# A macaron MoE–attention–MoE kernel: prefix sums in the other working bank, one more turn, and three operations moved between engines

## What is computed

```python
def ffn(x):                       # 8 experts of 384, 2 chosen per token, and one shared expert
    normed = layernorm(x) * ln_gamma + ln_beta
    logits = normed @ router_w.T
    top_v, top_i = top_k(softmax(logits), 2)
    gates = softmax(top_v)
    comb = sum(one_hot(top_i, 8) * gates[..., None], axis=1)
    out = sum(comb[:, e, None] * swiglu(normed, gate_up_w[e], down_w[e]) for e in range(8))
    return out + swiglu(normed, shared_gate_up_w, shared_down_w)

def attn(x):                      # windows of 128 tokens
    q, k, v = x @ Wq.T + bq, x @ Wk.T + bk, x @ Wv.T + bv
    scores = q @ k.T / sqrt(128)
    attn = softmax(where(in_top_32(scores), scores, -inf))
    r = leaky_relu(attn @ v) + x
    return layernorm(r) * gamma + beta

x = x + 0.5 * ffn(layernorm(x))
x = x + attn(layernorm(x))
x = x + 0.5 * ffn(layernorm(x))
```

## Time and profile before

| | us |
|---|---|
| median of three runs | 585.45 |
| span of the profiled execution, first to last instruction | 581.5 |
| median less span | 3.95 |
| PE busy | 500.6 (86%) |
| DVE busy | 388.7 (67%) |
| ACT busy | 330.0 (57%) |
| POOL busy | 332.0 (57%) |

### The profile page before, as it was taken

The page is one execution under the profiler, slowest core; times in us unless marked ns, Lnnn a source line. Parts: engine busy times, 40 slices in busy tenths (PEclk is TensorE's granted clock), DMA queues, the critical chain, the costliest instruction groups (busy, mean ns, idle before and its releaser), DMA issues.

```text
span 581.5 us, 14497 instructions
## 1 busy us (share of the span) xinstructions
PE 500.6 (86%) x3928; PEld 458.6 (79%) x3928; DVE 388.7 (67%) x1688; ACT 330.0 (57%) x792; POOL 332.0 (57%) x491
## 2 busy tenths in 40 slices
PE   2588999989999989999977499996899999799781
PEld 1466999979899989998974369794889989799780
DVE  5558864732558989879887958999785624222574
ACT  3367556565467777667753357673655546555430
POOL 2273766875565675356674405664566765565542
PEclk9989999999999999999977569997999999999996
DMA  6944858766886554766412254431668767676993
GB/s 184 316 112 167 261 188 237 243 233 239 284 260 218 190 187 173 258 226 205 155 47 59 69 195 176 160 112 54 209 224 257 248 221 246 228 262 237 322 320 124
DMA packets 88012, 117.82 MB, mean 203 GB/s; under 512 B 11848, under 2 KB 60880, under 8 KB 87936
## 3 DMA queue, kind: packets, MB, share of 16 engines
q1 hardware_dynamic: 76208, 96.75, 49.8%
q0 software_dynamic: 9312, 19.16, 9.5%
q10 hardware_dynamic: 2416, 0.99, 0.7%
HBM read 26.57 MB, written 26.19 MB: 91 GB/s over the span
## 4 chain that ended last, share of the span: by engine, by line
PE 52%; SPq 15%; ACT 9%; DMA 7%; issue 7%; DVE 5%; POOL 3%; ACTq 1%; POOLq 0%; DVEq 0%
PE ps_y L730 12%; PE ps_g L716 11%; PE ps_u L721 6%; SPq L441 6%; PE ps_h L721 5%; DMA xin<-rows 5%; SPq L484 4%; SPq L479 3%; PE ps_x L711 2%; PE w L630 2%; SPq L499 2%; POOL rows L1572 2%; ACT zz L849 2%; PE w L660 2%; PE w L616 2%
## 5 line engine op out<-in xcount | busy, mean ns | idle before, releaser
L1589 POOL DMA_INDIRECT results<-raw_gu,idx x163 | 164.6, 1010 | 144.8 <-ACT raw_gu L929 103.1
L1572 POOL DMA_INDIRECT rows<-zz,s_idx x128 | 126.0, 984 | 66.9 <-issue 28.3
L730 PE MATMUL ps_y<-dn_t,raw_gu 128*128 x978 | 139.2, 279 | 5.7 <-ACT raw_gu L929 5.0
L716 PE MATMUL ps_g<-x_t,raw_dn 128*128 128x128 f32 x978 | 137.5, 277 | 0.0
L730 PEld LDWEIGHTS ps_y<-dn_t,raw_gu 128*128 128x128 f32 x978 | 123.4, 193 | 9.3 <-issue 8.5
L716 PEld LDWEIGHTS ps_g<-x_t,raw_dn 128*128 128x128 f32 x978 | 122.8, 192 | 3.6 <-issue 3.5
L929 ACT COPY raw_gu<-ps_y 128x128 f32<-128x128 f32 x163 | 42.9, 263 | 103.5 <-PE ps_y L730 101.8
L923 ACT ACTIVATE sil<-ps_g 128x384 f32<-128x384 f32 x163 | 80.1, 491 | 22.0 <-PE ps_g L716 20.8
L920 ACT ACTIVATE x_t<-ps_x,bf_c,gf_c 128x128 f32<-128x128 f32 x163 | 75.3, 462 | 19.6 <-PE ps_x L711 19.4
L1397 DVE TENSOR_TENSOR raw_gu<-sil,ps_u 128x384 f32<-128x384 f32 x82 | 44.9, 548 | 54.2 <-PE ps_u L721 47.2
L1397 DVE TENSOR_TENSOR raw_gu<-sil,ps_h 128x384 f32<-128x384 f32 x81 | 44.5, 550 | 50.8 <-PE ps_h L721 35.9
(11 more groups left out here) (172 smaller groups left out, 729.0 us busy)
## 6 DMA issues: line engine op xcount, KB each, us to landing
raw_dn<-gu_t SPq DMA_DIRECT2D x163, 384.0 KB
xin<-rows SPq DMA_DIRECT2D x163, 64.5 KB
yg<-results SPq DMA_DIRECT2D x15, 512.0 KB, 5.1
results<-raw_gu,idx POOLq DMA_INDIRECT x163
rows<-pads SPq DMA_DIRECT2D x40, 64.5 KB
rows<-pads SPq DMA_DIRECT2D x5, 451.5 KB
rows<-zz,s_idx POOLq DMA_INDIRECT x128, 2.4
out<-xres SPq DMA_DIRECT2D x7, 256.0 KB, 3.3
```

Of the source, the lines that this page charges most:

```text
L716: t = pe.matmul(ps_g[k][:, c, :], ws[:, k4, c * P:(c + 1) * P], x_t[:, k, :], start=True, stop=True)
L730: t = pe.matmul(ps_y[:, 0, :], h_t[:, k4, c * P:(c + 1) * P], dn[:, bass.ds(off + c * D, D)], start=(c == 0), stop=(c == FC - 1))
L1572: pool.indirect_dma_start(xs, bass.IndirectOffsetOnAxis(s_idx[n][:, c, k:k + 1], 0), zz[n][:, k, c, :], None).then_inc(scat[n], 16)
L1589: pool.indirect_dma_start(yt, bass.IndirectOffsetOnAxis(idx[:, ky:ky + 1], 0), yb[:, ky, :], None).then_inc(yst[ky], 16)
```

## The change

- **Prefix sums.** Those of the first two steps go to bank `w0` (step 0 in its last quarter, step 1 in the one before), so they wait for no logits. `prefixes(0)` is issued ahead of `logits(1)`, `prefixes(1)` behind it.
- **One more turn.** `EMPTY_AT = (3,)` puts a turn without a search ahead of step 3. The turns are now (0,–,–,1), (1,0,–,2), (2,1,0,–), (–,2,1,–), (3,–,2,4), (4,3,–,5), (5,4,3,6), and on as before: eleven.
- **Gates.** In the first layer ACT multiplies the result rows by their gates (`gate`: eight operations of 128x128 for a step); DVE does the two adds (`add_gated`). The second layer keeps `combine`.
- **Values.** ACT copies `v` out of PSUM (128x512), POOL adds the bias in SBUF (128x512).
- **Beta.** POOL does `biased` (128x512).
- The numbers of `WEAVE` are new on all five engines.

```diff
-EMPTY_AT = ()
+EMPTY_AT = (3,)
...
     "sp": """
-        8 7 3 8 2 2 13 8 24 12 4 45 9 13 12 1 48 9 7 z1 14 22 38 4 4 z1 1 z1 5 z1 3 z6""",
+        15 1 15 z1 3 z1 7 5 29 6 6 49 2 6 26 z1 71 1 2 z1 15 6 44 1 6 z1 1 z1 2 4 3 z6""",
...
+        ps_pf_first = [w0[:, 3 - R, 0:(TB + 1) * NE].rearrange("p (t e) -> p t e", e=NE) for R in range(AHEAD)]
+
+        def prefix_of(R):
+            return ps_pf_first[R] if R < AHEAD else ps_pf
...
             def prefixes(R, listed):
 
                 pe.wait_ge(sel_done, R + 1)
                 if R >= AHEAD:
                     pe.wait_ge(shh, R + 2)
-                else:
-                    pe.wait_ge(lg_sb, AHEAD)
-                    prefixes_read(R)
-                pe.matmul(ps_pf, upper[:], sel[:, TB:, :], start=True, stop=False)
+                to = prefix_of(R)
+                pe.matmul(to, upper[:], sel[:, TB:, :], start=True, stop=False)
...
                 turn_z(R, R, 0, 0, 0)
                 turn()
+                prefixes(R - 1, R)
+                turn()
                 logits(R)
                 turn()
-            for R in range(AHEAD):
-                prefixes(R, R + 1)
-                turn()
+            prefixes(AHEAD - 1, AHEAD)
+            turn()
...
+            def values(a):
+                act.wait_ge(v_ps, a + 1)
+                act.copy(v[:], w1[:]).then_inc(v_cp, 1)
...
+            def gate(p):
+
+                act.wait_ge(gts, 1)
+                act.wait_ge(yld[p % 2], (p - p % 2) * 8 + 16)
+                for k in range(TB):
+                    for c in range(2):
+                        rows = yg[p % 2][:, k, c, :]
+                        act.activation(rows, rows, ACT.Copy, scale=gates[:, c, p * TB + k:p * TB + k + 1]).then_inc(gated, 1)
+                        turn()
...
+            def add_gated(p):
+
+                dve.wait_ge(gated, (p + 1) * 2 * TB)
+                xr = xres[:, p * TB:p * TB + TB, :]
+                for c in range(2):
+                    if c:
+                        dve.wait_ge(cb, p * N_CB + 2 * N_CB + 2)
+                    dve.tensor_tensor(xr, xr, yg[p % 2][:, :, c, :], ALU.add).then_inc(cb, 1 if c else 2)
+                    turn()
...
+            def values(a):
+                pool.wait_ge(v_cp, a + 2)
+                pool.tensor_tensor(v[:], v[:], wide(bv_b), ALU.add).then_inc(v_sb, 1)
+
+            def biased(a):
+
+                pool.wait_ge(xn_done, a * TB + TB)
+                xr = xres[:, a * TB:a * TB + TB, :]
+                pool.tensor_tensor(xr, xr, wide(ba_b), ALU.add).then_inc(xb_done, 1)
...
+                if a is not None:
+                    values(a)
+                    turn()
+                    biased(a)
+                    turn()
```

More of the change, by code:

```diff
@@ L131 @@
+        4 6 z1 4 z1 1 1 z1 1 5 z1 1 z1 1 z1 3 z1 2 5 z1 4 1 z1 2 1 2 z3 1 5 z2 1 z1 2 1 z4 3 z1 4 4 4 z1 3 2 z1 2 z1 1 z1 6 1 4 z1 8 1 2 z3 3 3 2 1
+        11 z4""",
 }
-VALUES, AFTER, AFTER_LATE, PICKS, SHARED, SHARED_LATE = 8, 13, 12, 19, 26, 31
+AFTER, AFTER_LATE, PICKS, SHARED, SHARED_LATE = 13, 12, 19, 26, 31
 def block_parts(ahead=True):
@@ L332, in macaron @@
             sem(n) for n in ("tl", "tl_e", "bl", "ended", "tab", "gts", "run0", "padded"))
-        cb = sem("cb")
+        cb, gated = sem("cb"), sem("gated")
         yld = [sem(f"yld{n}") for n in range(2)]
         yld_last = [[sem(f"yld_last{n}_{h}") for h in range(2)] for n in range(LAST_G)]
-        xn_done, xnT_ps, xnT_sb, q_ps, q_sb, k_ps, k_sb, v_ps, v_sb = (
-            sem(n) for n in ("xn_done", "xnT_ps", "xnT_sb", "q_ps", "q_sb", "k_ps", "k_sb", "v_ps", "v_sb"))
+        xn_done, xnT_ps, xnT_sb, q_ps, q_sb, k_ps, k_sb, v_ps, v_cp, v_sb = (
+            sem(n) for n in ("xn_done", "xnT_ps", "xnT_sb", "q_ps", "q_sb", "k_ps", "k_sb", "v_ps", "v_cp", "v_sb"))
         s_ps, sc_sb, tk, nm_done, ex_done, pr_done, ri_done, prT_ps, prT_sb, o_ps = (
@@ L961, in _ @@
                 if a in ALONE:
+                    gate(a)
                     norm_x(a, chain_alone[a])
@@ L968, in _ @@
                     turn()
+                    if p is not None:
+                        gate(p)
                 if a is not None:
@@ L1000, in _ @@
                     exps(a)
+                if s + 1 < len(TURNS) and TURNS[s + 1].a not in ALONE and TURNS[s + 1].p is not None:
+                    gate(TURNS[s + 1].p)
             gates_of_layer(1)
@@ L1181, in rows @@
                 if m == 0:
-                    t = dve.tensor_tensor(pos[:], ps_pf[:, 0:TB, :], tokens(run[:]), ALU.add)
+                    t = dve.tensor_tensor(pos[:], prefix_of(R)[:, 0:TB, :], tokens(run[:]), ALU.add)
                 elif m == 1:
-                    t = dve.tensor_tensor(run[:], run[:], ps_pf[:, TB, :], ALU.add)
+                    t = dve.tensor_tensor(run[:], run[:], prefix_of(R)[:, TB, :], ALU.add)
                 elif m == 2:
@@ L1324, in leaky @@
                 turn()
-            def wide(t):
-                return t[:].rearrange("p (o d) -> p o d", o=1).broadcast_to([P, TB, D])
-            def biased(A):
-                dve.wait_ge(xn_done, A * TB + TB)
-                xr = xres[:, A * TB:A * TB + TB, :]
-                dve.tensor_tensor(xr, xr, wide(ba_b), ALU.add).then_inc(xb_done, 1)
-                turn()
             def scaled(k, A):
@@ L1351, in attended @@
                 turn()
-            def values(a):
-                dve.wait_ge(v_ps, a + 1)
-                dve.tensor_tensor(v[:], w1[:], bv_b[:].rearrange("p (o d) -> p o d", o=1).broadcast_to([P, TB, D]),
-                                  ALU.add).then_inc(v_sb, 1)
             def search(a, between):
@@ L1484, in _ @@
                     stats_route(R, Jr, rt)
-                if A is not None:
-                    biased(A)
                 def between(m):
@@ L1491, in between @@
                         norms(m, chain_at[s], p, R)
-                    if m == VALUES and a is not None:
-                        values(a)
                     if m == after and A is not None:
@@ L1598, in _ @@
                 scatter(R, R % RING, turn)
+            pool.wait_ge(ld_c, 16 * 5)
             for a, A, J, *_ in TURNS:
+                if a is not None:
+                    values(a)
+                    turn()
+                    biased(a)
+                    turn()
                 if J is not None:
```

36 lines of the change are left out of this document (20 added, 16 removed).

## The result

The changed kernel takes 609.4 us (607.1 to 611.3) against 585.2: a ratio of 1.041, interval 1.037 to 1.045. It is slower by 24 us, where 579 was forecast and 592 was the range's end.

The account below looks back on a forecast made before the run. PE was taken to bound the full stretches, DVE's chain the layer change and J=4. Relief −14.3, start +4, empty turn +3, then −1.2 and +2 moved block 102 by −6.5: 585.45 to 579 us, range 567 to 592 (8 in 10).

Parts of the forecast that it names:

- the relief of 14.3 us: DVE up to the row numbers of J=4: gatings, value biases and betas taken away, 16.2 × 0.88 us, ends 8 and 16.2.
- POOL's adds: Sixteen 128x512 adds on POOL, at most 1.17 us each, said to fit; +2 us charged for bursts and delayed scatters.
- the start: First steps: PE waits for raw_dn, first prefix sum at 25.7 to 26.4; charged +4 us, ends −2 and +6.
- What bounds the kernel: PE from 54 to 285 and 354 to 384; DVE's chain to the block lists from 285 to 337 and 384 to 406.
- rival B: Slower: POOL's adds hold DVE, up to 13.4 us on the path to block 102; 587 to 597, best 592; chance 0.26.
- the lower end of 2.2 us for the first block: Start: the first block was to move by between 2.2 us and the whole shift of the first scatters.
- ACT's products: 64 gate products of 128x128 on ACT at 370 ns, 23.7 us in all, fitting except for bursts ahead of blocks.
- The empty turn: Turn without a search: brings J=2 and block 85 forward, but DVE loses work for its waits; +3 us, 0 to 5.
- The times given for J=2 (293) and block 85 (323): Layer change: row numbers of J=2 about 293 instead of 316.52, block 85 at 322 to 324 instead of 336.94.
- The sum: J=4 at 376.8, block 102 at 399.6 instead of 406.08; the −6.5 us passes to the end, giving 579.
- Rival A: Faster: DVE's waits shrink too, PE's own 382 plus the start's 4 sets block 102 at 385; 564 us; chance 0.13.

Follow-up runs that it names:

- adds back: The changed kernel with both bias adds (values and beta) back on DVE, without ACT's copy of v and POOL's sixteen adds: 595.9 us, ratio 1.021.
- adds alone: The kernel before with sixteen additional POOL adds of 128x512 on a tile nobody else uses, nothing waiting for them: 600.7 us, ratio 1.031.

## Why the prediction was wrong, step by step

Three terms of the sum failed: the relief of 14.3 us, of which the runs show almost nothing; POOL's adds, put at no cost to DVE, which cost 12 to 16 us; and the start, put at 4 us, which cost 10 to 12.

- **What bounds the kernel** was read rightly in the full stretches, and wrongly from 285 to 406. DVE busy for 88% of the time was taken for DVE setting the pace. But each engine's order is fixed, DVE's products of the blocks stand between the pieces of its own chain, and they wait for PE and ACT; a shorter chain waits longer there. The failed step is the factor in 16.2 × 0.88 = 14.3: with gatings and beta left out, 11.4 us of it up to J=4, the row numbers of J=4 come 0.8 us earlier instead of 10, and the end 2.3 us.
- **POOL's adds**: rival B was right in mechanism and nearly in size. It priced an add at 1.17 us and thirteen of them at 13.4 on the path; an add takes 1.27, holds DVE for 1.29, and sixteen cost 12 to 13.5 (adds back, DVE's relief taken off) to 16.4 us (adds alone). It got 0.26, and its 592 came out so low only because the relief of 14.3 stood against it. The row it rested on the earlier trace rows shows POOL giving way; in the changed kernel DVE gives way. The Trainium skill's page "SBUF — State Buffer", section "Who interferes with whom", states that the engine that issues first holds the shared ports and the other blocks. The trace agrees that one engine waits for the other's whole instruction, but its recorded starts do not show the order: DVE's add at 205.20 starts 0.50 us ahead of POOL's and is held all the same. The small TENSOR_SCALAR held for 1.24 us fits the same section, which counts that operation among those that can take the shared ports, under conditions that no run here tests. I read "a DVE operation with two SBUF inputs" as rare and short; the search, the route and the norms are full of them.
- **The start**: place and mechanism were right (PE waits 5.96 us for `raw_dn`), and the first sum came at 23.77, earlier than the 25.7 to 26.4 forecast. The term of +4 was mis-sized all the same: 10 to 12. It was read at the first block, which is not late at all, and not on the steps. By then PE had done less of the steps' work, and the third prefix sum came at 57.08 instead of 50.42; behind it the stage is full, as the text said itself. (The last of the sixteen scatters in before stood one row later than the one I took, at 43.05, and the lower end of 2.2 us for the first block does not follow from the 3.3 us hidden: 4.2 − 3.3 is 0.9. Its rows were requested 0.98 us later, 48.50 against 47.52.)
- **ACT's products** cost about what was said (392 ns each, 370 taken) and PE hardly waited for them; the wait that came instead, DVE's 14.0 us for ACT, was not on the list of what would be late next.
- **The empty turn** was charged with +3, measured 0 to 4. That J=4 and not J=2 sets what follows held. The times given for J=2 (293) and block 85 (323) did not: 318.75 and 346.20. Part of that is that all that lies ahead of them was late; but with the start of before and all three operations on DVE they still come at 302.12 and 330.59, 8 to 9 us later than forecast.
- **The sum**: start 10 to 12, turns 0 to 4, adds 12 to 14 (what little relief their move brought is in that) and gates 0 give 22 to 30 us; measured 24. The rivals were kept apart, each with the forecast's other terms, and no case had the start and the adds lose together; so the range ended at 592. (Rival A's 382 + 4 is 386, not 385; nothing hangs on it.)

## What to carry to other kernels

Busy share does not say that an engine sets the pace: where orders are fixed, ask at which waits a shorter chain would stop, and test it by leaving the work out before moving it. Elementwise work given to POOL was not taken from DVE here, which works on SBUF tiles beside it: each add cost DVE twice what it saved (1.29 us held for 0.68 saved). And a late start is to be measured at the chain of steps, not at the first block.

## What the runs showed of the hardware that was not expected

- POOL's adds hold DVE operations of a few elements to the add's end: 0.16 us became up to 1.84, and 2.84 beside two adds in a row. The held operation starts up to 0.6 us ahead of the add's recorded start and ends with it. MAX8 beside the same adds kept its 0.28 us.
- POOL's copy with one input (649 ns) holds DVE as well: sixteen copies cost 6.9 us, sixteen adds (1297 ns each) 16.4, about as their lengths.
- Products with a contraction of one row left PE busy, and yet the granted clock fell to 0.50 behind five of the eight groups that had them, and stayed at 1.00 behind one.
